# Attention, layer norm and a routed expert layer on one core: the four picked rows of a token summed as two halves inside the expert loop

## The chip, the cores and the metric

One core of a Trainium2 chip runs the whole program as one launch. The metric is the device time of an execution in microseconds (us). Between two versions, about 2% is what a measurement of this kernel can tell from no change.

## What is computed

4,096 tokens of width 256 go through one layer of attention with a residual and a layer norm, and then through a routed expert layer with a shared expert, a residual and a second layer norm. The reference, cut to the part that the change is about:

```python
topk_idx, topk_w = _route(tokens, router_weight, router_bias)    # 4 of 32 experts for each token
gate_vals = silu(einsum('th,eih->tei', tokens, gate_w))
up_vals = einsum('th,eih->tei', tokens, up_w)
expert_out = einsum('tei,ehi->teh', gate_vals * up_vals, down_w)
sel = take_along_axis(expert_out, topk_idx[:, :, None], axis=1)
mixed = (sel * topk_w[:, :, None]).sum(1)                        # the sum over a token's 4 picks
x = layernorm(x + mixed + shared)
```

## The kernel before

**Stages.** Attention, routing and the shared expert run over 8 chunks of 512 tokens, in an order written out by hand. Each token's row is scattered four times into a DRAM tensor `xs` (`expert_rows`), sorted by expert. Then comes the expert loop, and after it a closing stage that adds what is left of the picked rows, takes the moments and writes the output.

**The expert loop.** A tile is 128 rows of one expert. Two tiles are a pair, four are a group (`quad` in the code), which is thus two pairs, `par` 0 and `par` 1; below, a pair is also called half a group. There are 34 groups here. Buffers of a pair are double, chosen by `par`. For pair n the engines do this, each in its own program order:

- SP (`load_rows`, line 506) loads the two tiles of a pair into `xt[par]`, 132 KB each. It waits until pair n-2 has been transposed (`cX_ps`) and until DVE has copied that pair's ids and weights (`cmeta`).
- PE (`pairs`) transposes pair n+1 (line 1355), runs the 16 gate and up matmuls of pair n (line 996) and the down matmuls of pair n-1 (line 996).
- ACT (`pairs`) copies ids and weights (`keep_meta`, line 930), copies the transposed rows of pair n+1 (line 912), takes the silu of pair n (line 938) and scales the result of pair n-1 into `y_sb` (`copy_y`, line 921). `copy_y` waits until the scatter that last read this buffer, that of pair n-3, has landed (`y_scattered`).
- DVE (`pairs`) copies the ids and weights of pair n+1 (`copy_meta`, line 1825), multiplies silu by up (`hT`, line 1851), makes the ids of pair n-1 (`label_rows`, line 1842, which waits for the same scatter), then looks up the experts of pair n+2 in registers (`find_weights`, lines 295 and 1829) and copies their weights into `ws` (`copy_weights`, line 1834).
- POOL (`scatter_y`, line 608) scatters the two result tiles to the DRAM tensor `z` (`pick_rows`), four rows for each token.

**Early sums.** In the last 17 groups the loop also sums picked rows of the first 16 token tiles (of 32), one tile in each group: their results are known to be complete by then. `quads_with_ends` calls `load_early` on ACT behind each half of the groups from the 17th from the end to the second from the end; in half 0 it issues one DMA of 512 KB (line 951), 128 rows of 4 KB (four picks of 256 floats), into `early_z`, which lies over `wsgu_sb`. On DVE the function `beside` is called in `pairs` between `label_rows` and `find_weights`. `sum_halves(tile)` in half 1 of the same group waits for the load and adds 512 columns to 512 columns (line 1867). `sum_row(tile)` in half 0 of the next group adds 256 to 256 (line 1872), waits for that, and adds the result to the residual row in `sx` (line 1875). After the load of a tile the buffer is free once line 1867 has run (`e_free`), half a group before the next load.

The closing stage on DVE begins when all 16 tiles are summed (`e_sum`), and the picked rows of the other 16 tiles are loaded by SP after the loop (`load_picks`, line 525).

Of the kernel before, what the change touches and what calls it, by code (L numbers as in the profile page):

```python
# [9 lines left out]
ALU = mybir.AluOpType  # L10
# [3 lines left out]
P = 128  # L14
NTOK, DM = 4096, 256
# [5 lines left out]
TOPK, NGROUP = 4, 4  # L21
# [5 lines left out]
CT = 512  # L27
# [8 lines left out]
FIRST_TILES = FIRST_CHUNKS * TPC  # L36
# [34 lines left out]
SUM_LAG = 3  # L71
SUM_GROUPS = FIRST_TILES
# [12 lines left out]
def build(nc, xT, x, wqkv, wfc, wr, rbias, wsgu, wsd, wgu, wd, out):  # L85
# [7 lines left out]
    with ExitStack() as ctx:  # L93
# [6 lines left out]
        def sem(name):  # L100
            return ctx.enter_context(nc.semaphore(name))
# [140 lines left out]
        hT = [over(prod, 8 * DM + 4 * ROW + (4 + 2 * i) * P, 2 * P) for i in range(2)]  # L242
        ws = [over(prod, 8 * DM + 4 * ROW + 8 * P + i * 2 * KC * 2 * EI, 2, KC * 2 * EI) for i in range(2)]

        early_z = wsgu_sb.rearrange("p k c -> p (k c)")
        early_sum = wqkv_sb.rearrange("p k c -> p (k c)")[:, 2 * CT:2 * CT + 2 * DM]
        zt = {g: over(wgu_sb, (g - 5) * TPC * TOPK * DM, TPC * TOPK, DM).rearrange("p (t k) c -> p t k c", k=TOPK)
              for g in range(FIRST_CHUNKS + 1, CH)}
        zt[FIRST_CHUNKS] = over(stage.rearrange("p t k r -> p (t k r)"), 0, TPC * TOPK, DM)\
# [11 lines left out]
        b tabT tab_ready  # L261
        xt0 xt1 cX_ps cX_copied cmeta kept ws_ready ids_ready cgu_ps cth_ready ch_ready cy_ps cy_copied
        yscat0 yscat1
        e_free e_z e_half e_sum
        d_a d_ps dst_ready dmv_ready dveps_ready dstd_ready drstd_ready dnm_ready o2_ready stored""".split()
        S = {name: sem(name) for name in SEMS}
        xT_loaded = [S["xT_loaded0"], S["xT_loaded1"]]
# [1 line left out]
        scattered = [S[f"scat{i}"] for i in range(TPC)]  # L269
        xt_loaded = [S["xt0"], S["xt1"]]  # L270
        y_scattered = [S["yscat0"], S["yscat1"]]
        z_loaded = {g: [sem(f"z_loaded{g}_{t}") for t in range(TPC)] for g in range(FIRST_CHUNKS, CH)}

        NSMALL = 5 * 16
# [361 lines left out]
        def _(act):  # L636
# [305 lines left out]
                    first = isinstance(n, int) and n < 3  # L942
                    copy_y(n - 1, 1 - par, None if first else (quad * 32 if par else quad * 32 - 32))

            def load_early(quad, tile, par):
                if par:
                    return
                act.wait_ge(S["e_free"], tile + 1)
                for i in range(2):
                    act.wait_ge(y_scattered[i], quad * 32 - 32 * SUM_LAG)  # L950
                act.dma_start(early_z[:, :], z.rearrange("(n k) c -> n (k c)", k=TOPK)[bass.ds(tile * P, P), :])\
                    .then_inc(S["e_z"], 16)

            copy_xT(0, 0)
            quads_with_ends(act, quads, pairs, load_early)
# [466 lines left out]
        def _(dve):  # L1422
# [421 lines left out]
            def pairs(quad, par, has_prev, has_next, more=True, beside=None):  # L1844
                n = quad * 2 + par
                if has_next:
                    copy_meta(n + 1, 1 - par, quad + par)
                dve.wait_ge(S["cth_ready"], n + 1)
                if not (isinstance(n, int) and n < 2):
                    dve.wait_ge(S["cy_ps"], n - 1)  # L1850
                dve.tensor_tensor(hT[par][:, :], cth[par][:, :], banks[par][:, 2 * P:4 * P], ALU.mult)\  # L1851
                    .then_inc(S["ch_ready"], 1)
                if has_prev:
                    first = isinstance(n, int) and n < 3
                    label_rows(n - 1, 1 - par, None if first else (quad * 32 if par else quad * 32 - 32))
                if beside:
                    beside()
                if more:
                    found = find_weights(quad + 1, 2 * par)
                    dve.wait_ge(S["cgu_ps"], n + 1)  # L1860
                    copy_weights(par, found)

            def sum_halves(tile):
                dve.wait_ge(S["e_z"], tile * 16 + 16)
                if not isinstance(tile, int):
                    dve.wait_ge(S["e_sum"], tile)
                dve.tensor_tensor(early_sum[:, :], early_z[:, 0:2 * DM], early_z[:, 2 * DM:], ALU.add)\
                    .then_inc(S["e_free"], 1)

            def sum_row(tile):  # L1870
                dve.wait_ge(S["e_free"], tile + 2)
                dve.tensor_tensor(early_sum[:, 0:DM], early_sum[:, 0:DM], early_sum[:, DM:], ALU.add)\
                    .then_inc(S["e_half"], 1)
                dve.wait_ge(S["e_half"], tile + 1)
                dve.tensor_tensor(sx[:, bass.ds(tile * DM, DM)], sx[:, bass.ds(tile * DM, DM)], early_sum[:, 0:DM],
                                  ALU.add).then_inc(S["e_sum"], 1)

            dve.memset(slot_first[:, :], 0.0).then_inc(S["e_free"], 1)
            copy_meta(0, 0, 0)
            dve.wait_ge(S["big_w"], 16 * NBIG)  # L1880
            copy_weights(0, find_weights(0, 0))
            copy_weights(1, find_weights(0, 2))
            pairs(0, 0, False, True)
            pairs(0, 1, True, True)
            with dve.Fori(1, quads - SUM_START) as quad:
                pairs(quad, 0, True, True)
                pairs(quad, 1, True, True)
            first = dve.snap(dve.to_reg(quads - SUM_START))
            pairs(first, 0, True, True)
            pairs(first, 1, True, True, beside=lambda: sum_halves(0))  # L1890
            with dve.Fori(1, SUM_GROUPS) as tile:
                quad = dve.snap(dve.to_reg(quads - SUM_START + tile))
                pairs(quad, 0, True, True, beside=lambda: sum_row(tile - 1))
                pairs(quad, 1, True, True, beside=lambda: sum_halves(tile))
            pairs(quads - 1, 0, True, True, False, lambda: sum_row(SUM_GROUPS - 1))
            pairs(quads - 1, 1, True, False, False)
            label_rows(quads * 2 - 1, 1, None, True)


# [27 lines left out]
                dve.tensor_scalar(dveps[g][:, first:last], dmv[g][:, first:last, 1], EPS, None, ALU.add)\  # L1927
                    .then_inc(S["dveps_ready"], 1)

            dve.wait_ge(S["e_sum"], FIRST_TILES)  # L1930
            moments(0, 0, TPC)
            moments(1, 0, TPC)
            add_picks(4, range(TPC))
# [74 lines left out]
```

## Time and profile before

| | us |
|---|---|
| median of 3 runs | 597.07 |
| the runs | 588.22, 597.07, 598.96 |
| profiled execution, its own time | 589.56 |
| its span, first to last instruction | 587.8 |
| PE busy (matmuls) | 540.7 (92%) |
| DVE busy | 343.5 (58%) |
| ACT busy | 301.2 (51%) |
| POOL busy | 281.3 (48%) |

The profiled execution lies near the fastest of the three runs. Differences inside it are read against its own span; only at the end is the change carried over to the median. Busy shares are means over stages with different limits, so what matters below is read inside the expert loop, from about 316 us to about 547 us of the span. In a timeline row the first two numbers are the start and the duration in us; `x16` counts instructions merged into one row, and the bracket at its end gives how long the engine was idle before it and what ended that.

### The profile page before, as it was taken

To read this page: it belongs to the slowest core of one execution; us is meant where nothing else is said; L and a number is where in the kernel's file an instruction comes from. 1 tells how busy PE (TensorE), PEld (TensorE's weight loads), DVE (VectorE), ACT (ScalarE), POOL (GpSimd) and SP (SyncE) were. 2 spreads that over 40 slices of the span, in tenths; PEclk is the share of its full clock that TensorE was granted. 3 is DMA by queue.
4 is the path that set the end of the run, shared out by engine and by line. 5 is a ranking of instruction groups with operands and counts; after the bars stand their busy time and mean duration, and the time that the engine had idled before them with its cause. 6 is when DMAs were issued, how large, how long until landed. Compare 5 with 4: busy or idle time off the path is not lost.

```text
span 587.8 us, 16300 instructions
## 1 busy us (share of the span) xinstructions
PE 540.7 (92%) x4820; PEld 418.7 (71%) x4821; DVE 343.5 (58%) x1167; ACT 301.2 (51%) x641; POOL 281.3 (48%) x293
## 2 busy tenths in 40 slices
PE   5989999999999999999888999999988888888894
PEld 2445668677666766775437999999977777778783
DVE  2032647697985987678834444444455555555865
ACT  1324462766747665343214666666555555545454
POOL 5000000564677766667741666666655555555400
PEclk9989999999999999999988999999999999989999
DMA  7999987897799799799523454555666666667498
GB/s 258 248 220 229 249 237 192 246 282 223 245 259 288 243 311 398 272 383 344 183 92 91 136 159 160 163 168 179 200 209 213 212 203 213 209 201 254 162 383 293
DMA packets 125821, 135.35 MB, mean 230 GB/s; under 512 B 76872, under 2 KB 107087, under 8 KB 125136
## 3 DMA queue, kind: packets, MB, share of 16 engines
q1 hardware_dynamic: 105984, 87.53, 50.8%
q0 software_dynamic: 12672, 34.10, 15.3%
q10 hardware_dynamic: 7120, 13.13, 7.2%
q8 instruction: 27, 0.44, 0.3%
q14 instruction: 18, 0.15, 0.1%
HBM read 74.79 MB, written 60.96 MB: 231 GB/s over the span
## 4 chain that ended last, share of the span: by engine, by line
PE 56%; DMA 21%; issue 6%; DVE 4%; SPq 4%; POOL 3%; ACT 3%; DVEq 1%; ACTq 1%; POOLq 0%
PE bank L996 51%; DMA prod<-expert_rows 4%; DMA o_slots<-wgu_sb 4%; DMA pick_rows<-prod,ids 4%; PE bank L1355 4%; DMA wd_sb<-o_slots 3%; DMA wgu_sb<-pick_rows 3%; DMA wsgu_sb<-pick_rows 2%; POOL expert_rows L574 1%; ACT sx L965 1%; SPq L364 1%; SPq L355 1%; POOL pick_rows L608 1%; SPq L525 1%; PE bank L1044 1%
## 5 line engine op out<-in xcount | busy, mean ns | idle before, releaser
L608 POOL DMA_INDIRECT pick_rows<-prod,ids x134 | 133.6, 997 | 114.5 <-ACT prod L921 68.8
L574 POOL DMA_INDIRECT expert_rows<-stage,pos x128 | 128.6, 1004 | 57.3 <-issue 35.0
L996 PE MATMUL bank<-prod 128*128 128x128 f32 x1088 | 135.2, 278 | 1.0 <-DVE prod L1834 1.0
L996 PEld LDWEIGHTS bank<-prod 128*128 128x128 f32 x1088 | 128.9, 194 | 1.6 <-ACT prod L912 1.2
L996 PE MATMUL bank<-wd_sb,wqkv_sb 128*128 128x512 f32 x192 | 92.1, 616 | 7.0 <-DMA wqkv_sb<-in_wqkv 6.2
L1834 DVE COPY prod<-wgu_sb 128x512 f32 x136 | 52.8, 430 | 62.2 <-issue 42.0
L921 ACT ACTIVATE prod<-bank,kept 128x256 f32<-128x256 f32 x136 | 57.0, 470 | 50.0 <-PE bank L996 27.2
L996 PE MATMUL bank<-wd_sb,prod 128*128 x272 | 70.9, 384 | 1.3 <-DVE prod L1851 1.3
L996 PEld LDWEIGHTS bank<-wgu_sb 128*32 128x32 f32 x2048 | 58.7, 136 | 17.5 <-issue 14.2
L996 PE MATMUL bank<-wgu_sb 128*32 128x64 f32 x2048 | 65.8, 296 | 2.9 <-DMA wgu_sb<-k_slots 2.9
L996 PEld LDWEIGHTS bank<-wd_sb,wqkv_sb 128*128 128x128 f32 x192 | 35.3, 196 | 42.5 <-issue 36.4
L1355 PE MATMUL bank<-ident,prod 128*128 128x128 f32 x272 | 42.1, 278 | 19.1 <-DMA prod<-expert_rows 17.0
L567 POOL TENSOR_TENSOR rstdt<-vepst,neg_half 128x4 f32<-128x4 f32 x8 | 9.0, 1129 | 99.7 <-DVE vepst L1456 99.7
L1355 PEld LDWEIGHTS bank<-ident,prod 128*128 128x128 f32 x272 | 33.0, 143 | 31.6 <-issue 22.2
L1851 DVE TENSOR_TENSOR prod<-prod,bank 128x256 f32<-128x256 f32 x68 | 28.5, 419 | 42.0 <-ACT prod L938 41.8
L996 PEld LDWEIGHTS bank<-wd_sb,prod 128*128 128x128 f32 x272 | 47.0, 193 | 5.4 <-issue 1.7
L996 PE MATMUL bank<-prod,wsgu_sb 128*128 128x512 f32 x96 | 45.2, 618 | 3.4 <-DVE hsT L1523 3.4
L938 ACT ACTIVATE prod<-bank 128x256 f32<-128x256 f32 x68 | 26.0, 383 | 42.5 <-PE bank L996 41.9
L912 ACT ACTIVATE prod<-bank 128x512 f32<-128x512 f32 x68 | 40.6, 597 | 3.5 <-PE bank L1355 2.9
L1474 DVE TENSOR_REDUCE smax<-bank 128x32 f32<-128x512 f32 x16 | 10.9, 681 | 48.0 <-PE bank L996 48.0
L653 ACT ACTIVATE stage<-sx 128x1024 f32<-128x1024 f32 x32 | 34.1, 1065 | 9.3 <-DMA expert_rows<-stage,pos 6.7
L996 PEld LDWEIGHTS bank<-prod,wsgu_sb 128*128 128x128 f32 x96 | 18.2, 197 | 24.8 <-issue 19.6
(168 smaller groups left out, 699.2 us busy)
## 6 DMA issues: line engine op xcount, KB each, us to landing
prod<-expert_rows SPq DMA_DIRECT2D x136, 132.0 KB
wsgu_sb<-pick_rows ACTq DMA_DIRECT2D x16, 512.0 KB
wgu_sb<-pick_rows SPq DMA_DIRECT2D x12, 512.0 KB, 11.0
wgu_sb<-in_wgu SPq DMA_DIRECT2D x2, 2560.0 KB, 13.0
expert_rows<-pad_rows SPq DMA_DIRECT2D x4, 1056.0 KB, 19.4
wd_sb<-in_xT SPq DMA_DIRECT2D x8, 512.0 KB, 4.8
q_slots<-wd_sb SPq DMA_DIRECT2D x16, 256.0 KB, 4.2
k_slots<-wd_sb SPq DMA_DIRECT2D x16, 256.0 KB
```

The source lines that it names most:

```text
L567: pool.tensor_tensor(rstdt[:, :], vepst[:, :], neg_half[:, :], ALU.pow).then_inc(S["rstd_ready"], 1)
L574: pool.indirect_dma_start(xs, bass.IndirectOffsetOnAxis(ap=pos[e % 2][:, i, k:k + 1], axis=0), stage[:, i, k, :], None, bounds_check=XROWS ...
L608: pool.indirect_dma_start(z, bass.IndirectOffsetOnAxis(ap=index[:, j:j + 1], axis=0), rows[:, j, :], None, bounds_check=TOPK * NTOK - 1, o ...
L653: act.activation(stage[:, i, :, 0:DM], x1_of(e)[:, i, :].unsqueeze(1).broadcast_to([P, TOPK, DM]), ACT.Copy)
L912: act.activation(xtT[par][:, :], banks[2][:, :], ACT.Copy).then_inc(S["cX_copied"], 1)
L921: last = act.activation(to[:, j, :], banks[6 + par][:, j * DM:(j + 1) * DM], ACT.Copy, scale=kept[par][:, j, 1:2])
L938: act.activation(cth[par][:, :], banks[par][:, 0:2 * P], ACT.Silu)\
L996: return pe.matmul(dst, lhsT, rhs, start=(k == 0), stop=(k == n - 1))
L1355: last = pe.transpose(banks[2][:, c:c + P], xt[par][:, j, k * P:(k + 1) * P], ident[:, :])
L1474: dve.tensor_reduce(smax[:, hf, :], score_view(hf), AX, ALU.max).then_inc(S["smax"], 1)
L1834: last = dve.tensor_copy(ws[par][:, j, :], wgu_sb[:, bass.ds(found[j], KC * 2 * EI)])
L1851: dve.tensor_tensor(hT[par][:, :], cth[par][:, :], banks[par][:, 2 * P:4 * P], ALU.mult)\
```

## The change

`early_z` becomes two buffers of 512 columns, each for two of the four picks of a row. `load_early` now issues a DMA in both halves of a group, 256 KB each (128 rows of 2 KB). `sum_halves` and `sum_row` are replaced by `sum_half`, called in both halves: it waits for its load, adds 256 columns to 256, waits for that, and adds the result to the row in `sx`. The sums of a tile now stand in the group behind the one in which its loads are issued, each in the same half as its load was, so a load is waited for one whole group later. The load of tile t waits until `sum_half` of tile t-1 has read the buffer, which happens in the same half group. Columns added and bytes loaded are the same in all. On DVE the group that stood by itself (`first`) is gone and the last half of the last group now has a sum.

```diff
-        early_z = wsgu_sb.rearrange("p k c -> p (k c)")
-        early_sum = wqkv_sb.rearrange("p k c -> p (k c)")[:, 2 * CT:2 * CT + 2 * DM]
+        early_z = [over(wsgu_sb.rearrange("p k c -> p (k c)"), h * 2 * DM, 2, DM) for h in range(2)]
+        early_sum = wqkv_sb.rearrange("p k c -> p (k c)")[:, 2 * CT:2 * CT + DM]
...
-            def load_early(quad, tile, par):
-                if par:
-                    return
-                act.wait_ge(S["e_free"], tile + 1)
-                for i in range(2):
-                    act.wait_ge(y_scattered[i], quad * 32 - 32 * SUM_LAG)
-                act.dma_start(early_z[:, :], z.rearrange("(n k) c -> n (k c)", k=TOPK)[bass.ds(tile * P, P), :])\
-                    .then_inc(S["e_z"], 16)
+            def load_early(quad, tile, half):
+                act.wait_ge(S["e_half"], tile * 2 + half)
+                if half == 0:
+                    for i in range(2):
+                        act.wait_ge(y_scattered[i], quad * 32 - 32 * SUM_LAG)
+                act.dma_start(early_z[half][:, :, 0:DM],
+                              z.rearrange("(n k) c -> n k c", k=TOPK)[bass.ds(tile * P, P),
+                                                                      2 * half:2 * half + 2, :])\
+                    .then_inc(early_landed[half], 16)
...
-            def sum_halves(tile):
-                dve.wait_ge(S["e_z"], tile * 16 + 16)
-                if not isinstance(tile, int):
-                    dve.wait_ge(S["e_sum"], tile)
-                dve.tensor_tensor(early_sum[:, :], early_z[:, 0:2 * DM], early_z[:, 2 * DM:], ALU.add)\
-                    .then_inc(S["e_free"], 1)
-
-            def sum_row(tile):
-                dve.wait_ge(S["e_free"], tile + 2)
-                dve.tensor_tensor(early_sum[:, 0:DM], early_sum[:, 0:DM], early_sum[:, DM:], ALU.add)\
+            def sum_half(tile, half):
+                dve.wait_ge(early_landed[half], tile * 16 + 16)
+                dve.wait_ge(S["e_sum"], tile * 2 + half)
+                dve.tensor_tensor(early_sum[:, :], early_z[half][:, 0, 0:DM], early_z[half][:, 1, 0:DM], ALU.add)\
                     .then_inc(S["e_half"], 1)
-                dve.wait_ge(S["e_half"], tile + 1)
-                dve.tensor_tensor(sx[:, bass.ds(tile * DM, DM)], sx[:, bass.ds(tile * DM, DM)], early_sum[:, 0:DM],
+                dve.wait_ge(S["e_half"], tile * 2 + half + 2)
+                dve.tensor_tensor(sx[:, bass.ds(tile * DM, DM)], sx[:, bass.ds(tile * DM, DM)], early_sum[:, :],
                                   ALU.add).then_inc(S["e_sum"], 1)
...
-            with dve.Fori(1, quads - SUM_START) as quad:
+            with dve.Fori(1, quads - SUM_GROUPS) as quad:
                 pairs(quad, 0, True, True)
                 pairs(quad, 1, True, True)
-            first = dve.snap(dve.to_reg(quads - SUM_START))
-            pairs(first, 0, True, True)
-            pairs(first, 1, True, True, beside=lambda: sum_halves(0))
-            with dve.Fori(1, SUM_GROUPS) as tile:
-                quad = dve.snap(dve.to_reg(quads - SUM_START + tile))
-                pairs(quad, 0, True, True, beside=lambda: sum_row(tile - 1))
-                pairs(quad, 1, True, True, beside=lambda: sum_halves(tile))
-            pairs(quads - 1, 0, True, True, False, lambda: sum_row(SUM_GROUPS - 1))
-            pairs(quads - 1, 1, True, False, False)
+            with dve.Fori(0, SUM_GROUPS - 1) as tile:
+                quad = dve.snap(dve.to_reg(quads - SUM_GROUPS + tile))
+                pairs(quad, 0, True, True, beside=lambda: sum_half(tile, 0))
+                pairs(quad, 1, True, True, beside=lambda: sum_half(tile, 1))
+            pairs(quads - 1, 0, True, True, False, lambda: sum_half(SUM_GROUPS - 1, 0))
+            pairs(quads - 1, 1, True, False, False, lambda: sum_half(SUM_GROUPS - 1, 1))
             label_rows(quads * 2 - 1, 1, None, True)
```

## Rows read from the trace of the kernel before

**Rows 1.** The page: the span.
```profile
span 587.8 us, 16300 instructions
```

**Rows 2.** Windows: us, busy us of PE, PEld, DVE, ACT, POOL (instructions), clock, DMA share, GB/s.
```profile
330.00:348.50 18.50, 18.50 (x146) 17.59 (x145) 8.03 (x31) 11.77 (x31) 11.67 (x12) 1.00 0.47 148
...
488.00:503.00 15.00, 12.81 (x96) 11.61 (x96) 8.08 (x26) 8.06 (x21) 8.29 (x9) 1.00 0.68 214
```

**Rows 3.** The tile `wsgu_sb` (`early_z`): shortest, median, longest ns, first and last start in us.
```profile
L951 ACTq DMA_DIRECT2D wsgu_sb<-pick_rows x16: 344/344/372, 421.8 to 535.1; - x16
```

**Rows 4.** Timeline of PE without early loads: transposes of two pairs.
```profile
384.08 0.60 PE L1355 MATMUL bank<-ident,prod 128*128 128x128 f32 x4
...
387.17 0.60 PE L1355 MATMUL bank<-ident,prod 128*128 128x128 f32 x4
```

**Rows 5.** Timeline of DVE without early loads.
```profile
383.92 0.42 DVE L1851 TENSOR_TENSOR prod<-prod,bank 128x256 f32<-128x256 f32 x1 [0.99 <-ACT prod L938]
...
386.01 0.16 DVE L1825 COPY meta<-prod 128x4 f32<-128x4 f32 x1
386.92 0.42 DVE L1851 TENSOR_TENSOR prod<-prod,bank 128x256 f32<-128x256 f32 x1 [0.74 <-ACT prod L938]
```

**Rows 6.** Timeline of DVE with early loads: a group, and one later row.
```profile
481.26 0.42 DVE L1851 TENSOR_TENSOR prod<-prod,bank 128x256 f32<-128x256 f32 x1 [0.94 <-ACT prod L938]
...
482.25 0.43 DVE L1875 TENSOR_TENSOR sx<-sx,wqkv_sb 128x256 f32 x1 [0.17 <-DVE wqkv_sb L1872]
483.85 0.78 DVE L1834 COPY prod<-wgu_sb 128x512 f32 x2 [1.17 <-PE bank L996]
484.55 0.15 DVE L1825 COPY meta<-prod 128x4 f32<-128x4 f32 x1
484.61 0.41 DVE L1851 TENSOR_TENSOR prod<-prod,bank 128x256 f32<-128x256 f32 x1
...
486.07 0.69 DVE L1867 TENSOR_TENSOR wqkv_sb<-wsgu_sb 128x512 f32<-128x512 f32 x1 [0.97 <-DMA wsgu_sb<-pick_rows]
...
488.29 0.16 DVE L1825 COPY meta<-prod 128x4 f32<-128x4 f32 x1
...
537.34 0.83 DVE L1834 COPY prod<-wgu_sb 128x512 f32 x2 [1.48 <-issue]
```

**Rows 7.** Waits from 421 to 548 us: us in total, times, longest us.
```profile
ACT prod L921 <- DMA pick_rows<-prod,ids: 22.5, 16, 2.8
...
PE bank L1355 <- DMA prod<-expert_rows: 16.7, 13, 2.2
...
DVE wqkv_sb L1867 <- DMA wsgu_sb<-pick_rows: 6.0, 7, 1.3
```

**Rows 8.** Timeline of PE with early loads: transposes.
```profile
481.42 0.60 PE L1355 MATMUL bank<-ident,prod 128*128 128x128 f32 x4
...
493.30 0.65 PE L1355 MATMUL bank<-ident,prod 128*128 128x128 f32 x4 [1.74 <-DMA prod<-expert_rows]
```

**Rows 9.** The chain that ended last, with early loads: start us, us from issue to landing.
```profile
472.62 5.22 DMA pick_rows<-prod,ids
...
489.31 3.86 DMA prod<-expert_rows
...
515.38 2.26 DMA prod<-expert_rows
```

**Rows 10.** DMA from 421 to 536 us: a queue's share of 16 engines' time; issues.
```profile
q1 hardware_dynamic: 8674, 8.15, 24.8%
q10 hardware_dynamic: 2160, 7.87, 23.7%
...
prod<-expert_rows SPq DMA_DIRECT2D x61, 132.0 KB
```

**Rows 11.** The page, costliest groups: busy us, mean ns of one | idle us before, releaser.
```profile
L608 POOL DMA_INDIRECT pick_rows<-prod,ids x134 | 133.6, 997 | 114.5 <-ACT prod L921 68.8
...
L921 ACT ACTIVATE prod<-bank,kept 128x256 f32<-128x256 f32 x136 | 57.0, 470 | 50.0 <-PE bank L996 27.2
```

More of the change, by code:

```diff
@@ L263, in build @@
         yscat0 yscat1
-        e_free e_z e_half e_sum
+        e_z0 e_z1 e_half e_sum
         d_a d_ps dst_ready dmv_ready dveps_ready dstd_ready drstd_ready dnm_ready o2_ready stored""".split()
@@ L271, in build @@
         y_scattered = [S["yscat0"], S["yscat1"]]
+        early_landed = [S["e_z0"], S["e_z1"]]
         z_loaded = {g: [sem(f"z_loaded{g}_{t}") for t in range(TPC)] for g in range(FIRST_CHUNKS, CH)}
@@ L1861, in pairs @@
                     copy_weights(par, found)
-            def sum_halves(tile):
-                dve.wait_ge(S["e_z"], tile * 16 + 16)
-                if not isinstance(tile, int):
-                    dve.wait_ge(S["e_sum"], tile)
-                dve.tensor_tensor(early_sum[:, :], early_z[:, 0:2 * DM], early_z[:, 2 * DM:], ALU.add)\
-                    .then_inc(S["e_free"], 1)
-            def sum_row(tile):
-                dve.wait_ge(S["e_free"], tile + 2)
-                dve.tensor_tensor(early_sum[:, 0:DM], early_sum[:, 0:DM], early_sum[:, DM:], ALU.add)\
+            def sum_half(tile, half):
+                dve.wait_ge(early_landed[half], tile * 16 + 16)
+                dve.wait_ge(S["e_sum"], tile * 2 + half)
+                dve.tensor_tensor(early_sum[:, :], early_z[half][:, 0, 0:DM], early_z[half][:, 1, 0:DM], ALU.add)\
                     .then_inc(S["e_half"], 1)
-                dve.wait_ge(S["e_half"], tile + 1)
-                dve.tensor_tensor(sx[:, bass.ds(tile * DM, DM)], sx[:, bass.ds(tile * DM, DM)], early_sum[:, 0:DM],
+                dve.wait_ge(S["e_half"], tile * 2 + half + 2)
+                dve.tensor_tensor(sx[:, bass.ds(tile * DM, DM)], sx[:, bass.ds(tile * DM, DM)], early_sum[:, :],
                                   ALU.add).then_inc(S["e_sum"], 1)
-            dve.memset(slot_first[:, :], 0.0).then_inc(S["e_free"], 1)
+            dve.memset(slot_first[:, :], 0.0).then_inc(S["e_half"], 1)
             copy_meta(0, 0, 0)
@@ L1928, in moments @@
                     .then_inc(S["dveps_ready"], 1)
-            dve.wait_ge(S["e_sum"], FIRST_TILES)
+            dve.wait_ge(S["e_sum"], 2 * FIRST_TILES)
             moments(0, 0, TPC)
```

## Prediction

> **What bounds the kernel now.** I read the page first: PE is busy 92% of a span of 587.8 us [rows 1], so the question is where in the expert loop it is not. The windows answer that [rows 2]. Without early loads PE is busy for all of 18.50 us at a DMA share of 0.47; with them it is busy 12.81 of 15.00 us at 0.68. The timeline gives the pace of the undisturbed stretch: transposes of successive pairs start 387.17 - 384.08 = 3.09 us apart [rows 4], so a group takes 6.18 us and PE sets it. With early loads the 16 DMAs run from 421.8 to 535.1 us [rows 3], 113.3 us for 15 groups or 7.55 us each. A group with an early load therefore costs 1.37 us more than one without, 15 x 1.37 = 20.6 us in all. That is everything the change can win back in these groups.
>
> The waits tell who stands still in that stretch [rows 7]: `copy_y` on ACT for a scatter (22.5 us in 16 waits), PE's transposes for expert rows (16.7 us in 13), and DVE's line 1867 for the early load itself (6.0 us in 7). The totals overlap in time and may not be added. The timelines show how they hang together. DVE waits 0.97 us for the early load at 486.07 and so copies ids and weights (`copy_meta`) only at 488.29 [rows 6]. SP may load into that buffer only after this copy, and its second DMA is out at 489.31; it takes 3.86 us [rows 9], beside an early load, and PE stands 1.74 us before it transposes at 493.30 [rows 8]. The reader is to see that DVE is off PE's path only while `copy_meta` comes early enough.
>
> **The loop that sets the pace.** From a pair's transposes to those three pairs later, with the rows of before: transposes to `hT` 484.61 - 481.42 = 3.19; `hT` to `copy_meta` 488.29 - 484.61 = 3.68; `copy_meta` to the last issue 489.31 - 488.29 = 1.02; landing 3.86; then 0.13 to 493.30. The sum is 11.88 us, as measured [rows 6, 8, 9], instead of 3 x 3.09 = 9.27. Undisturbed it is 386.92 - 384.08 = 2.84, 386.01 - 383.92 = 2.09, 1.02, 2.26 for a landing that met little traffic [rows 9] and 0.13: 8.34 us, a slack of 0.93 us [rows 4, 5].
>
> **The change, part by part.**
>
> *The wait for the load goes.* The early load is waited for a group later. The longest idle time seen for it is 1.3 us [rows 7], so 6 to 7 us more notice covers it, and the 256 KB loads are no longer than the 512 KB ones. Removed: up to 6.0 us of DVE idle time; what of this reaches PE is in the loop sum below, not on top of it.
>
> *DVE's work.* Before, one half of a group has one add of 512 columns (0.69 us), the other two adds of 256 (0.42 and 0.43) with a wait of 0.17 between [rows 6]. After, both halves have the latter. The first form cost little when its data were there. The second is heavy: with `sum_row`, `hT` to `copy_meta` takes 484.55 - 481.26 = 3.29 us, against 2.09 without [rows 5, 6], as the register work for the next weights is not hidden behind the adds (1.17 us idle before line 1834). `hT` to the next `hT` is 484.61 - 481.26 = 3.35 us, which is more than PE's 3.09. So DVE alone holds each of these halves at 3.35 us or more, a group at 6.70. That is the lower bound. The upper one is a longer register stretch: 1.48 us instead of 1.17 at 537.34 [rows 6] makes 3.66. One more wait against a register in each half lies between these.
>
> *The loads.* Early loads take 23.7% of 115 us x 16 engines, 27.3 us for 15 of them: 1.8 us of all engines each. The expert rows take 24.8%, 28.5 us for 61 DMAs of 132 KB, 0.47 us each, and so 0.91 us per 256 KB in packets of 1 KB [rows 10]. Two halves with packets of 2 KB then cost the engines the same 1.8 us as one whole; no bytes are saved. What changes is the burst. A load of expert rows issued beside a whole one takes 3.86 us instead of 2.26, +1.6; beside a half I take half of that, 3.06 us, for every pair now instead of mostly every second. The bounds are 2.26 (it slips past) and 3.86 (no relief).
>
> *The pace after.* The loop is 2.84 + 3.29 + 1.02 + 3.06 + 0.13 = 10.34 us for three pairs, 3.45 us a pair. With a landing of 2.26 it is 3.18, so DVE's 3.35 holds; with 3.86 it is 3.71. As DVE's floor and this loop lie 0.1 us apart and each has scatter, I take 3.50: a group of 7.00 us, 0.55 less than now.
>
> *The scatters.* `copy_y` and `label_rows` wait for scatters that take up to 5.22 us beside a whole load [rows 9]. Beside a half one, the same +0.9 of engine time instead of +1.8 brings them down to about 4.3. Ahead of the landing stand two copies of 0.47 us and two issues of 1.0 us [rows 11], an estimated 2.9 us, so the slowest would need 7.2 us of a two-pair time of 7.0, the others less. I count nothing for it beyond the 3.50.
>
> *What ACT waits for.* Each early load now waits for the first add on DVE in the same half. That ends at 482.25 - 0.17 = 482.08, 0.82 us behind the start of `hT` [rows 6], while ACT has its two copies of 0.47 us to do [rows 11]. Behind it on ACT are `keep_meta`, the copy of the transposed rows and the next silu; POOL and PE wait for those. ACT's 8.06 us busy of 15.00 [rows 2] is the cover; without it the price is what DVE is late, some 0.1 to 0.3 us a half. The additional 16 issues (0.34 us each [rows 3]) run while ACT's datapath copies: nothing.
>
> *Ends.* The first group with loads now has no sums; it had about 6.2 us already: nothing. The last group gets sums in both halves, but its last `label_rows` needs only be ready when the down matmuls and `copy_y` are: nothing, or the two adds and their wait, 1.0 us, if that cover is gone. One group less written out on DVE: nothing.
>
> **Sum.** 15 x (7.55 - 7.00) = 8.3 us less: span 579.5, own time 589.56 - 8.3 = 581.3, that is -1.4%. The profiled execution was 7.5 us faster than the median of the runs, 597.07. Carried over, 597.07 - 8.3 = 588.8; I say 589.
>
> The Trainium skill, page "DMA: Bandwidth & Descriptors", section "Bandwidth", speaks against this change: batch DMAs to 1 MiB or more, since a DMA costs about 2.0 us plus its bytes at 436 GB/s. By that, 512 KB in one takes an estimated 3.2 us and in two 5.2, and if the fixed part held the engines the change would cost 2.0 us a group. The trace doesn't bear that out: DMAs of 132 KB hold the engines for 0.47 us each, so the fixed part must be latency, which is hidden here.
>
> **Rivals.**
>
> 1. *Almost the whole loss goes.* Half bursts fall below the slack of 0.93 us and DVE's register work hides behind its waits; a group takes 6.2 to 6.5 us. For it: half of +1.6 is 0.8, below 0.93. Against it: `copy_meta` itself comes 1.2 us later in each half, and 3.35 us is a plain row. Saves 15 x 1.2 = 18: 579 on the median.
> 2. *Nothing changes.* The bytes are the same and the DMA share of 0.68 is what sets the pace; `copy_y` waits move to other places. For it: 22.5 us of waits for scatters, no part of DVE. A group stays at 7.4 to 7.6: 595 to 598.
> 3. *Slower: DVE becomes the bound.* The place is the stretch between `label_rows` and `copy_meta`, in each half; it decides from 7.55 / 2 = 3.78 us per half. The rows give 3.35 to 3.66; a scatter waited for in `label_rows` in front of it adds directly, as there is no light half left in which DVE catches up. At 3.95 us a group takes 7.90: +5 us, 602.
> 4. *Small DMAs hold the engines* (the engines busy 2.0 us more a group than the 1.8 above): with a DMA share of 0.68 + 2.0 / 7.55 = 0.94 nothing would be left for scatter, and a group would take at least 1 to 2 us more: 612 to 627. Only engine times of 0.47 us for 132 KB stand against it, and they do so plainly.
>
> **Chances.** Forecast (4 to 12 us less) 0.54, rival 1 0.12, rival 2 0.20, rival 3 0.12, rival 4 0.02. About 2%, 12 us, is what a measurement of this kernel can tell from no change. Faster by more than that takes rival 1 and DVE's floor of 3.35 (15 x 0.85 = 12.8 us): 0.12 + 0.13 = 0.25. Slower by over 2% is rival 4 and the tail of rival 3, with the runs of before 11 us apart: 0.08. The rest, 0.67, lies within. The range: below, rival 1 all but its end, 577; above, rival 3, 602. Forecast's own: 585 to 593.
>
> **What would show it.** Right: no row of DVE waiting for the early load; issues of early loads 3.5 us apart; `hT` to `hT` of 3.35 us or more with hardly any idle time for silu; PE's waits for expert rows many and short (0.3 to 0.4 us) instead of 13 long ones; expert rows landing in about 3.1 us. Wrong: landings near 3.9 us, waits of `copy_y` for scatters still at 22 us, or `hT` to `hT` above 3.78 us. The same DMA share with two queues' times unchanged would confirm the cost of the loads; a share above 0.8 would refute it.

## The result

| | before | changed |
|---|---|---|
| median of 20 runs, us | 596.84 | 584.82 |
| lowest to highest, us | 588.22 to 601.75 | 582.45 to 590.98 |
| ratio of the runs | | 0.9886, 95% interval 0.9846 to 0.9925 |
| profiled execution's span, us | 587.8 | 584.4 |

The changed kernel is about 1.1% faster, clear of chance and inside the 2% that stood for "no change". In a second comparison the ratio was 0.9866 (0.9817 to 0.9915). The two medians lie 2.0% apart, more than the ratio says: the ratio compares the means of the fast runs alone, those within 1.5% of their kernel's fastest, which leaves out 9 of the 20 runs of before and none of the changed kernel. The two first traces lie only 3.4 us (0.6%) apart. Part of the kernel before's spread is what its stalls do to TensorE's clock, which comes below; its first trace had little of that.

**The profile after.** First the early loads (tile `wsgu_sb`: count, shortest, median and longest ns, first and last start in us) and the first add that reads them:

```profile
L951 ACTq DMA_DIRECT2D wsgu_sb<-pick_rows x32: 339/344/363, 423.1 to 535.4; - x32
L1868 DVE TENSOR_TENSOR wqkv_sb<-wsgu_sb x32: 411/419/426, 429.4 to 543.6; 128x256 f32<-128x256 f32 x32
```

From the first to the last of 32 loads there are 15.5 groups: (535.4 - 423.1) / 15.5 = 7.24 us a group, instead of 7.55 [rows 3]. The forecast was 7.00. From here on the pace of a group is worked out like this for every kernel with early loads.

These means hide how unlike the groups of the kernel before are. Here are its issues of early loads, one for each group, and below them those of half 0 in the changed kernel (timelines of ACT):

```profile
421.82 0.36 ACTq L951 DMA_DIRECT2D wsgu_sb<-pick_rows  x1
428.00 0.35 ACTq L951 DMA_DIRECT2D wsgu_sb<-pick_rows  x1
436.79 0.34 ACTq L951 DMA_DIRECT2D wsgu_sb<-pick_rows  x1
442.99 0.37 ACTq L951 DMA_DIRECT2D wsgu_sb<-pick_rows  x1
451.69 0.34 ACTq L951 DMA_DIRECT2D wsgu_sb<-pick_rows  x1
```

```profile
439.18 0.34 ACTq L951 DMA_DIRECT2D wsgu_sb<-pick_rows  x1
...
446.21 0.34 ACTq L951 DMA_DIRECT2D wsgu_sb<-pick_rows  x1
...
453.56 0.34 ACTq L951 DMA_DIRECT2D wsgu_sb<-pick_rows  x1
```

In the kernel before, short and long groups take turns: 6.18, 8.79, 6.20, 8.70 us, and so on to the end. The short ones run at the pace without early loads (6.18); the loss of 1.37 us a group is one of about 2.6 us in every second group. The changed kernel has nearly even groups: of the 15 from one issue in half 0 to the next, the median is 7.03 us and the longest 9.01. This was not in the forecast, which took 7.55 us as the time of each group.

The waits from 421 to 548 us (total us, times, longest us), which answer to [rows 7]:

```profile
PE bank L1357 <- DMA prod<-expert_rows: 10.3, 15, 1.7
ACT prod L922 <- DMA pick_rows<-prod,ids: 8.8, 7, 3.3
DVE ids L1844 <- DMA pick_rows<-prod,ids: 6.2, 4, 2.6
```

No row is left in which DVE waits for an early load; it was 6.0 us. PE's waits for expert rows fell from 16.7 to 10.3 us, `copy_y`'s for scatters from 22.5 to 8.8. New are waits of ACT ahead of `keep_meta`, two rows of which are these:

```profile
ACT kept L931 <- issue: 8.5, 6, 1.8
ACT kept L931 <- DMA pick_rows<-prod,ids: 7.3, 11, 1.2
```

With the two other rows of that line they come to 25.2 us in 31 waits, against 1.7 us in 5 before. An ACT that is late by itself also has less to wait for in `copy_y`.

The timeline of DVE, two halves of a group, answers to [rows 6]:

```profile
438.05 0.42 DVE L1853 TENSOR_TENSOR prod<-prod,bank 128x256 f32<-128x256 f32 x1
...
439.02 0.43 DVE L1871 TENSOR_TENSOR sx<-sx,wqkv_sb 128x256 f32 x1
440.89 0.76 DVE L1836 COPY prod<-wgu_sb 128x512 f32 x2 [1.44 <-PE bank L998]
441.57 0.22 DVE L1827 COPY meta<-prod 128x4 f32<-128x4 f32 x1
441.64 0.41 DVE L1853 TENSOR_TENSOR prod<-prod,bank 128x256 f32<-128x256 f32 x1
...
444.01 0.76 DVE L1836 COPY prod<-wgu_sb 128x512 f32 x2 [1.10 <-PE bank L998]
444.88 0.17 DVE L1827 COPY meta<-prod 128x4 f32<-128x4 f32 x1
```

`hT` to `copy_meta` takes 441.57 - 438.05 = 3.52 us in one half and 444.88 - 441.64 = 3.24 in the other, where the forecast had 3.29 for both. The idle time in front of line 1836, in which DVE looks up the experts in registers, is longer in half 0 (1.44 us, against 1.10). The row names PE, but the matmuls that this line waits for are those that `hT` needed already.

The DMA queues from 421 to 536 us answer to [rows 10], and the chain (start us, us) to [rows 9]:

```profile
q1 hardware_dynamic: 9092, 8.89, 29.5%
q10 hardware_dynamic: 4453, 8.11, 23.4%
```

```profile
477.55 3.60 DMA prod<-expert_rows
...
491.92 2.54 DMA prod<-expert_rows
```

Queue q10 took 23.4% of the engines' time for 8.11 MB; before it was 23.7% for 7.87 MB. So two DMAs of 256 KB in packets of 2 KB cost the engines what one of 512 KB did, as forecast, and small transfers do not hold them. The queue of the expert rows, q1, did not stay the same. From 428 to 528 us, where it carries nothing else, it took 28.2% of the engines' time for 7.30 MB, against 24.7% for 7.18 MB in the kernel before: 14% more time for 2% more bytes.

### The profile page after: what moved, and what is told of

It reads as the page before. It is cut to its first block, busy times and chain, and to the rows that moved or that the text cites. A ratio compares the mean times of both kernels' runs of the same rounds, so it can differ in the third digit from the quotient of the medians.

```text
span 584.4 us, 16411 instructions
## 1 busy us (share of the span) xinstructions
PE 542.0 (93%) x4820; PEld 419.2 (72%) x4821; DVE 346.0 (59%) x1183; ACT 299.5 (51%) x641; POOL 281.2 (48%) x293
## 4 chain that ended last, share of the span: by engine, by line
PE 59%; DMA 17%; issue 7%; SPq 4%; POOL 4%; DVE 3%; ACT 2%; DVEq 2%; POOLq 0%; ACTq 0%
PE bank L998 54%; DMA prod<-expert_rows 5%; PE bank L1357 4%; POOL expert_rows L575 4%; DMA o_slots<-wgu_sb 3%; DMA wd_sb<-o_slots 2%; DMA wgu_sb<-pick_rows 2%; DMA pick_rows<-prod,ids 1%; ACT sx L967 1%; SPq L514 1%; SPq L356 1%; DMA expert_rows<-stage,pos 1%; DVEq L296 1%; DMA wqkv_sb<-in_wqkv 1%; PE bank L1046 1%
## 5 line engine op out<-in xcount | busy, mean ns | idle before, releaser
L1836 DVE COPY prod<-wgu_sb 128x512 f32 x136 | 54.1, 440 | 67.9 <-issue 52.0
```

Of the source, the lines that this page charges most:

```text
L1836: last = dve.tensor_copy(ws[par][:, j, :], wgu_sb[:, bass.ds(found[j], KC * 2 * EI)])
```

## The experiments

Ratios are against the kernel before on the same chip, with 95% intervals. PE's busy time is that of the 100 us from 428 to 528 us of each trace; matmuls at a low clock count in full. "Single groups" are the shortest, the median and the longest of the 15 between issues of early loads (of half 0, where there are two). The kernel with sums only has no such issues: its groups are counted from add to add, which takes in the last group, 8.88 us. Counted so, the changed kernel is at (543.6 - 429.4) / 15.5 = 7.37 us.

| kernel | ratio (95%) | median us | us per group | single groups | PE busy |
|---|---|---|---|---|---|
| before, first trace | | 596.84 | 7.55 | 6.18, 6.40, 10.42 | 85.1 |
| before again | 1.0031 (0.9991 to 1.007) | 598.36 | 7.83 | 6.18, 6.86, 10.73 | 85.9 |
| changed, first trace | 0.9886 (0.9846 to 0.9925) | 584.82 | 7.24 | 6.66, 7.03, 9.01 | 89.1 |
| changed again | 0.9866 (0.9817 to 0.9915) | 585.65 | 7.21 | 6.64, 7.05, 8.56 | 89.7 |
| halves, old notice | 0.9899 (0.9851 to 0.9947) | 588.90 | 7.37 | 6.18, 7.44, 8.26 | 87.1 |
| whole, a group's notice | 0.989 (0.9845 to 0.9934) | 587.25 | 7.35 | 6.66, 7.13, 9.42 | 87.8 |
| halved loads, no sums | 0.9885 (0.9812 to 0.9959) | 587.99 | 7.34 | 6.61, 7.17, 8.31 | 88.2 |
| whole loads, no sums | 1.0013 (0.9969 to 1.0057) | 596.67 | 7.81 | 6.18, 7.76, 9.99 | 83.5 |
| sums, no loads | 0.9782 (0.972 to 0.9844) | 579.73 | 6.99 | 6.66, 6.94, 8.88 | 95.2 |
| adds apart | 0.9917 (0.9884 to 0.995) | 588.88 | 7.33 | 6.45, 7.36, 8.17 | 86.5 |
| changed + tile scatters | 0.98 (0.9742 to 0.9858) | 582.25 | 7.10 | 6.68, 7.03, 7.51 | 90.6 |
| adds apart + tile scatters | 0.9818 (0.9766 to 0.987) | 583.68 | 6.90 | 6.21, 6.81, 7.98 | 92.5 |
| before + tile scatters | 0.9925 (0.9885 to 0.9965) | 589.69 | 7.66 | 6.22, 6.44, 10.78 | 85.3 |

### The two kernels again

No edit: the kernel before and the changed one beside it.

> The kernel before once more, beside itself: what difference two equal kernels show here, and a second trace of it. Ratio 1.00, within 1% either way; its runs lie between 588 and 602 us. In its trace the groups with an early load take 7.4 to 7.8 us each (7.55 in the first trace); if they take over 7.8 us, the first trace was one of the quick executions and the change is worth more than its two traces show.

> The changed kernel once more, on the same chip as the three others. Theory (the wait for the early load is gone and the bursts are halved): ratio 0.98 to 0.99, groups of 7.0 to 7.3 us in its trace. Rival (nothing but chance of one execution): ratio 0.995 or more.

Two equal kernels differed by 0.3%. The second trace of before has a span of 598.2 us against 587.8 of the first and 7.83 us a group; the changed kernel's second trace has 583.3 us and 7.21. The change is thus worth 0.3 to 0.6 us a group by the traces, depending on which execution of before is taken.

Part of what makes before vary shows in its windows (length, busy us of PE, PEld, DVE, ACT, POOL, granted clock, DMA share, GB/s), here of its second trace:

```profile
498.00:501.50 3.50, 1.06 (x8) 0.66 (x8) 2.03 (x6) 0.97 (x3) 0.98 (x1) 1.00 0.96 334
501.50:505.00 3.50, 3.50 (x19) 3.43 (x18) 0.88 (x3) 0.82 (x3) 2.05 (x2) 0.51 0.39 113
...
515.00:518.60 3.60, 1.38 (x11) 0.98 (x11) 2.02 (x6) 1.31 (x4) 0.98 (x1) 1.00 0.92 329
518.60:522.00 3.40, 3.40 (x17) 3.22 (x16) 1.05 (x4) 0.70 (x2) 1.07 (x1) 0.50 0.43 129
```

and in the timeline of PE of the same trace:

```profile
500.86 0.65 PE L1355 MATMUL bank<-ident,prod 128*128 128x128 f32 x4 [2.44 <-DMA prod<-expert_rows]
501.35 3.44 PE L996 MATMUL bank<-prod 128*128 128x128 f32 x16
...
505.63 0.60 PE L1355 MATMUL bank<-ident,prod 128*128 128x128 f32 x4
506.07 1.95 PE L996 MATMUL bank<-prod 128*128 128x128 f32 x16
```

PE stands 2.44 us for expert rows, while the DMA share is 0.96, and in the stretch behind that the granted clock is 0.51: the lower of its two levels, 1.2 instead of 2.4 GHz. Sixteen matmuls take 3.44 us instead of 1.95. The same happens at 518.6 and at 535.7 us in this trace, and once in the first trace of before, at 524.6 us (0.51, after an idle time of 2.09 us). Each costs about 1.7 us on top of the stall: 2.80 + 1.88 us of matmuls instead of 1.95 + 1.03 in the first trace. The groups show the same price: with a drop they take 10.42 to 10.73 us, without one the long ones take 8.44 to 8.98. In neither trace of the changed kernel does the clock drop between 421 and 540 us; PE's longest idle time there is 1.69 us. Outside this stretch it does: near 312 to 317 us in both traces, as in the first trace of before, and at 542 us in the second. The runs bear out that the clock is part of before's spread: of the 57 runs of before that the ratios below rest on, the lowest third (592.4 us on the mean) had a mean granted clock of 0.984, the highest (597.8 us) one of 0.979. This was not in the forecast.

### Notice without halves, halves without notice

```diff
 # halves, old notice: the changed kernel, half 0 added in half 1 of the same group, half 1 in half 0 of the next
-                pairs(quad, 0, True, True, beside=lambda: sum_half(tile, 0))
-                pairs(quad, 1, True, True, beside=lambda: sum_half(tile, 1))
+                pairs(quad, 0, True, True, beside=lambda: sum_half(tile - 1, 1))
+                pairs(quad, 1, True, True, beside=lambda: sum_half(tile, 0))
```

> The changed kernel with only the point of adding moved back: two loads of 256 KB as after the change, each added half a group later as before (half 0 in half 1 of the same group, half 1 in half 0 of the next). The number of adds on DVE is that of the change. If the halved bursts bring the gain: ratio 0.985 to 0.99, like the changed kernel, since a load of 256 KB lands in 2.5 to 3.9 us and half a group is 3.5 us, so DVE waits little. If the longer notice brings it: DVE waits 0.3 us or more in most halves, and the ratio is 0.995 to 1.01.

```diff
 # whole, a group's notice: the kernel before, both sums in the group behind the load
-                pairs(quad, 0, True, True, beside=lambda: sum_row(tile - 1))
-                pairs(quad, 1, True, True, beside=lambda: sum_halves(tile))
+                pairs(quad, 0, True, True, beside=lambda: sum_halves(tile))
+                pairs(quad, 1, True, True, beside=lambda: sum_row(tile))
```

> The kernel before with only the point of adding moved: one load of 512 KB a group as before, its first add (512 columns) in half 0 of the next group and the other two in half 1, so that the load has a whole group. DVE's work is that of the kernel before. If the longer notice brings the gain: ratio 0.985 to 0.99 or better, since DVE has one light half. If the halved bursts bring it: ratio 0.995 to 1.005, expert rows still landing in 3.9 us beside each load, and only the 6.0 us of DVE's waits for the early load gone from the waits.

Each part alone brings most of the gain, 1.0% and 1.1%, and both together 1.1 to 1.3%; the intervals of all overlap. In both kernels the ratio is the one expected if the part tested brings the gain, so neither is the only cause, and the parts are not additive. That both relieve the same loop, once by making DVE punctual, once by making the traffic smoother, is a reading that no run separates. The single groups add something to it: with whole loads and a group's notice short and long groups no longer take turns (6.66 to 7.33 us for 11 of 15), with halves and the old notice they still do for the most part (6.2 to 7.4 and 7.6 to 8.3). With halves and the old notice DVE also still waits for its loads:

```profile
DVE wqkv_sb L1868 <- DMA wsgu_sb<-pick_rows: 6.3, 9, 3.8
```

### Loads alone, sums alone

```diff
 # halved loads, no sums (whole loads: the same edit in the kernel "whole, a group's notice")
-                dve.tensor_tensor(early_sum[:, :], early_z[half][:, 0, 0:DM], early_z[half][:, 1, 0:DM], ALU.add)\
-                    .then_inc(S["e_half"], 1)
-                dve.wait_ge(S["e_half"], tile * 2 + half + 2)
-                dve.tensor_tensor(sx[:, bass.ds(tile * DM, DM)], sx[:, bass.ds(tile * DM, DM)], early_sum[:, :],
-                                  ALU.add).then_inc(S["e_sum"], 1)
+                dve.memset(slot_first[:, 0:1], 0.0).then_inc(S["e_half"], 1)
+                dve.memset(slot_first[:, 1:2], 0.0).then_inc(S["e_sum"], 1)
 # sums, no loads
-                act.dma_start(early_z[half][:, :, 0:DM], ...)
-                dve.wait_ge(early_landed[half], tile * 16 + 16)
```

> The changed kernel with the sums left out: the 32 loads of 256 KB stay, the two adds of each half are replaced by two writes of one column, so the early token tiles lack their picked rows. It shows what the halved loads cost without DVE's work. If the loads (not DVE) hold the loop: groups stay at 6.9 to 7.3 us, ratio 0.985. If DVE's stretch from hT to copy_meta holds it (theory: 1.2 us later against a slack of 0.93): hT to copy_meta falls to about 2.3 us and groups to 6.2 to 6.4 us, ratio about 0.97.

> The same without the sums, but with the 16 loads of 512 KB, waited for a group later: the early token tiles lack their picked rows. Beside the halved loads it shows the burst alone. If a whole burst is worth a stall of its own: groups 0.3 us or more longer than with halves, expert rows beside it landing in 3.9 us against 3.1. If the slack of 0.93 us covers both, no difference between the two, both near 6.2 to 6.4 us.

> The changed kernel with its early loads left out: DVE adds what lies in the buffer, so the early token tiles get wrong picked rows. It shows DVE's work without the traffic. Theory (DVE's floor): groups of 6.7 to 6.8 us, hT to hT 3.35 us, PE with idle time of some 0.3 us a half; ratio 0.98. Rival (only the traffic costs): groups 6.2 us, ratio 0.965 to 0.97.

These three take the loss apart. The sums without traffic need 6.99 us a group ((537.0 - 428.7) / 15.5 from line 1863, the first add), with a median of 6.94, near the forecast floor of 6.70; the timeline of DVE shows where the rest is:

```profile
483.66 0.42 DVE L1849 TENSOR_TENSOR prod<-prod,bank 128x256 f32<-128x256 f32 x1
...
487.05 0.42 DVE L1849 TENSOR_TENSOR prod<-prod,bank 128x256 f32<-128x256 f32 x1
...
490.56 0.42 DVE L1849 TENSOR_TENSOR prod<-prod,bank 128x256 f32<-128x256 f32 x1
```

`hT` to `hT` is 3.39 and 3.51 us: 3.35 and a little more. That the rest is one more wait against a register and lookups that vary is likely, but not shown.

The halved loads without any sums need 7.34 us, hardly less or more than the whole change. Taking most of 1 us of DVE's work out of each half gained nothing: of the two expectations that came true in which the loads hold the loop, not the 6.2 to 6.4 us of the other. The waits of that kernel point to what held it:

```profile
ACT prod L922 <- DMA pick_rows<-prod,ids: 31.1, 20, 2.9
DVE ids L1844 <- DMA pick_rows<-prod,ids: 18.9, 17, 2.3
```

`copy_y` and `label_rows` wait for scatters. DVE's waits only moved from its own work to the landings. The whole loads without sums are at 7.81 us and at the time of the kernel before (ratio 1.0013), and the granted clock drops in that trace too (0.96 on the mean of 428 to 528 us, with 1.00 for the halves), three times, after PE had stood 2.94, 2.69 and 2.48 us:

```profile
428.00:528.00 100.00, 83.48 (x602) 75.64 (x601) 38.46 (x152) 49.97 (x127) 51.08 (x52) 0.96 0.67 207
```

Between whole and halved bursts, with no sums in either, lie 0.47 us a group and 1.3% by the ratios (medians 587.99 and 596.67 us, intervals that do not touch: 0.9812 to 0.9959 and 0.9969 to 1.0057). The burst is a cause of its own. At about 1.7 us each, the three clock drops are an estimated 0.3 of the 0.47 us: most of what the whole burst costs here goes through the clock.

### The adds taken apart

```diff
 # adds apart: first add ahead of hT, second behind label_rows
                 if has_next:
                     copy_meta(n + 1, 1 - par, quad + par)
+                if beside:
+                    add_half(*beside)
                 dve.wait_ge(S["cth_ready"], n + 1)
...
                 if beside:
-                    beside()
+                    add_sum(*beside)
```

> The changed kernel with the two adds of a half taken apart: the first stands ahead of the hT multiply, where DVE waits for silu anyway, the second behind label_rows, so that no completion is waited for between them and the register work runs while the second add does. Same adds, same loads. Theory: hT to copy_meta falls from 3.3 to about 2.5 us and groups from 7.1 to about 6.5 us; 15 x 0.6 = 9 us, ratio 0.97 against before. Rival (the traffic holds the loop, not DVE): groups stay at 7 us or more, ratio 0.985.

The rival won. `hT` to `copy_meta` did fall (a half at 485.64 to 487.95, 2.31 us), but the group stayed at 7.33 us. The trace of this kernel shows the loop that holds it without DVE's work in the way (timelines of POOL and ACT):

```profile
484.10 0.97 POOL L609 DMA_INDIRECT pick_rows<-prod,ids  x1 [1.80 <-ACT prod L922]
485.37 1.20 POOL L609 DMA_INDIRECT pick_rows<-prod,ids  x1 [0.30 <-issue]
```

```profile
482.41 0.47 ACT L922 ACTIVATE prod<-bank,kept 128x256 f32<-128x256 f32 x1 [1.70 <-DMA pick_rows<-prod,ids]
...
482.78 0.47 ACT L922 ACTIVATE prod<-bank,kept 128x256 f32<-128x256 f32 x1
...
489.57 0.47 ACT L922 ACTIVATE prod<-bank,kept 128x256 f32<-128x256 f32 x1 [1.50 <-DMA pick_rows<-prod,ids]
```

```profile
485.37 4.17 DMA pick_rows<-prod,ids
```

ACT begins `copy_y` at 482.41, is done at 483.25, POOL issues the first scatter at 484.10 and the second at 485.37, that one lands 4.17 us later (the chain's row), and ACT begins the next copy into the same buffer at 489.57. Those are 7.16 us for two pairs, which is a group: 2.96 up to the last issue, 4.17 for the landing and 0.03 until the next copy.

### A semaphore for each tile's scatter

```diff
 # tile scatters: copy_y waits, and POOL issues, for each of the two tiles by itself
-                if old is not None:
-                    act.wait_ge(y_scattered[par], old)
                 for j in range(2):
-                    last = act.activation(to[:, j, :], banks[6 + par][:, j * DM:(j + 1) * DM], ACT.Copy,
-                                          scale=kept[par][:, j, 1:2])
-                last.then_inc(S["cy_copied"], 1)
+                    if old is not None:
+                        act.wait_ge(y_scattered[par][j], old)
+                    act.activation(to[:, j, :], banks[6 + par][:, j * DM:(j + 1) * DM], ACT.Copy,
+                                   scale=kept[par][:, j, 1:2]).then_inc(S["cy_copied"], 1)
...
-                wait_apart(pool, S["cy_copied"], pair * 2 + par + 1)
                 for j in range(2):
+                    wait_apart(pool, S["cy_copied"], pair * 4 + par * 2 + j + 1)
```

> The changed kernel with the scatter of each result tile on a semaphore of its own: copy_y waits for the scatter of the tile that it overwrites only, and POOL issues a tile's scatter when that tile is copied, not when both are. This shortens the loop copy, issue, landing, copy by one copy (0.84 - 0.2 us) without touching DVE or the early loads. Theory A (the scatters' loop of 7.2 us for two pairs holds the changed kernel, DVE's 6.9 stands right behind it): groups fall from 7.2 to 6.9 or 7.0 us, ratio about 0.98 against before. Theory B (only DVE's stretch holds it): no difference to the changed kernel, 0.987. Theory C (POOL's added waits make its issues later): ratio 0.99 or more.

> The same with the adds taken apart as in adds_apart, so that both loops are shorter: scatters' 6.4 to 6.5 us for two pairs, DVE's about 5.5 to 6.2 us a group. Theory A: groups of 6.5 to 6.8 us, 15 x 0.5 = 7 us below the changed kernel, ratio 0.975 against before. If neither loop is what holds it but the traffic itself: groups stay at 7.1 to 7.4 us, ratio 0.99 as adds_apart.

> The kernel before with the scatters on a semaphore for each tile, and nothing else. If the scatters' loop was already what one half of the loss in the kernel before came from (copy_y waited 22.5 us for scatters there, landings of 5.2 us beside a whole load make a loop of 8.2 us): groups fall from 7.55 by some 0.3 us, ratio 0.985 to 0.99. If the expert rows, held back by DVE, set the pace alone: ratio 0.995 to 1.005.

With the adds apart the shorter scatter loop takes a group from 7.33 to 6.90 us and the ratio from 0.9917 to 0.9818; the intervals (0.9884 to 0.995, 0.9766 to 0.987) do not touch. `copy_y`'s waits for scatters go from 32.0 us to nearly nothing:

```profile
ACT prod L924 <- DMA pick_rows<-prod,ids: 1.9, 5, 0.6
```

So the scatters' loop held that kernel, in every group: the median falls from 7.36 to 6.81 us. The 6.5 to 6.8 us a group and the ratio of 0.975 that were expected were not quite reached.

On the changed kernel the same edit takes a group from 7.2 to 7.10 us and gives 582.25 us, ratio 0.98 (0.9742 to 0.9858): the fastest kernel here that computes the whole result, though its interval overlaps that of the changed kernel. The median of its groups, 7.03 us, is that of the changed kernel; what is gone is the long group near the start. On the kernel before it gives 0.9925, below 1 by its interval, although the pace in its one trace (7.66 us, two clock drops in it) is not below the 7.55 and 7.83 of the two traces of before. `copy_y`'s waits for scatters fall there from 22.5 to 6.6 us, but short and long groups still take turns. That scatters cost the kernel before something is thus supported by the time and not by the pace of the trace.

## Why the prediction was right, and where it was off

- **What could be won, 1.37 us a group.** Right as a mean; it is 2.6 us in every second group of the kernel before and nothing in the others. No kernel went below a mean of 6.90 us a group.
- **The wait for the load goes.** Right: no such wait is left. The longer notice taken alone (whole, a group's notice) is worth most of the gain, which fits a loss that runs through a late `copy_meta`.
- **DVE's floor of 3.35 us a half.** Nearly right: 3.39 to 3.51 in the kernel without loads, a median of 6.94 us a group instead of 6.70. The term is mis-sized by 0.1 us a half; the extra wait that had been named and not counted may be the reason.
- **The loads cost the engines the same.** Right: 23.4% for 8.11 MB against 23.7% for 7.87 MB, though the expert rows' queue took more time for each byte than before. The "Bandwidth" section of the Trainium skill's page "DMA: Bandwidth & Descriptors", on batching to 1 MiB, was weighed and set aside, and the runs bear that out: the halved bursts beat the whole ones by 1.3% with no sums beside them. The cost of about 2.0 us plus the bytes that the prediction names with it stands in another section of that page, "Anatomy of one DMA — SWDGE (gpsimd) path", for DMAs issued from GpSimd; the early loads are issued from ACT. The section "Queues, rings and completion order" of the same page says that an engine takes turns between queues by the packet, a packet there being some 9 to 17 descriptors. Whether the packets of 2 KB and 4 KB that the profile counts are of that kind is shown by no run here, so that rule stays unproven as the reason.
- **Expert rows landing in 3.06 us.** Not borne out where it can be seen: the eight landings of expert rows in the chain from 421 to 540 us take 2.30 to 3.93 us, 3.33 on the mean, and the seven of the kernel before 2.26 to 4.01, 3.43 on the mean. These are only those that something waited for. PE's waits did not become many and short as forecast either: 15 of 0.7 us on the mean, the longest 1.7.
- **The pace, 3.50 us a pair.** Right for the typical group: the median is 7.03 and 7.05 us in the two traces, 3.52 a pair. The means, 7.24 and 7.21, lie above it through single long groups, 9.01 and 8.56 us near the start and some of 7.5 to 7.9. The term that was too small is the one on the scatters, "I count nothing for it", and with it the landing of "about 4.3". In the long group of the first trace a scatter landed in 5.19 us and `label_rows` stood for it (the chain, then the timeline of DVE):

```profile
429.74 5.19 DMA pick_rows<-prod,ids
```

```profile
435.01 0.17 DVE L1844 CAST ids<-kept 128x2 uint32<-128x2 f32 x1 [1.85 <-DMA pick_rows<-prod,ids]
```

- **The scatters' loop.** The forecast's own sum, 2.9 + 4.3 = 7.2 us for the slowest, was measured as 7.16, but in the kernel with the adds apart, where this loop holds every group. In the changed kernel nine of 15 groups are shorter than that, so there it can hold some and not the typical one; DVE's 6.94 us comes nearest to the 7.03.
- **ACT's wait on the first add.** It does occur: ACT stands 25.2 us ahead of `keep_meta`, which follows `load_early` in its program, instead of 1.7. How much of it is the first add is unclear. The profile's view of line 1868 puts 8.1 us in 6 waits down to it, its rows of line 931 only 1.8 in 2. The 7.3 us put down to scatters need not be that either, as `load_early` asks only for scatters of three groups earlier. The kernel with sums only has 17.0 us of this idle time and is the fastest of all; the one with the adds apart has 7.6, gained nothing by it, and waits 32.0 us for scatters in `copy_y` instead. The wait was not taken away by itself, so its cost stays open, and so does that of the 16 more issues, which the forecast put at nothing.
- **The sum.** 8.3 us less were forecast. The ratio, 0.9886, is 6.8 us of 592.7, the mean of before that it rests on; the medians differ by 12.0 us. For the profiled execution 581.3 us was forecast and 586.14 measured, 3.4 less instead of 8.3. The traces' pace gives 15 x (7.55 - 7.24) = 4.7 us from the first two traces and 15 x (7.83 - 7.21) = 9.3 from the second two. In these stand one and three clock drops of before, an estimated 1.7 and 5.1 us; without them the change saves 3.0 and 4.2 us. So the loops that the forecast reasons about gave a third to a half of what it promised, and the clock, of which it says nothing, gave 1.7 to 5.1 us on top. That the total came out near 8.3 us is in part luck, and the step that the median moves by what the quick execution moves did not hold.
- **Rivals.** "Almost the whole loss goes" fell on DVE's floor; "nothing changes" was half right in its mechanism (the scatters) and wrong in its result; "DVE becomes the bound" was right about the place and wrong about the result: DVE's typical 6.94 us lies just below the 7.03 measured; "small DMAs hold the engines" did not occur.

**What stays open.** In both traces of the changed kernel and in that with whole loads and a group's notice, one group near the start of the sums takes 8.6 to 9.4 us. In the changed kernel's first trace it goes with the scatter that lands in 5.19 us; why that one lands so late is not known. Why short and long groups take turns in the kernel before is not shown either. And why the halved loads without sums are no faster in ratio than the full change (0.9885 and 0.9886), although they lack DVE's work, is explained by the scatters' loop only as far as one trace shows. Group times, waits and clock drops of the experiments come from one trace each.

## What to carry to other kernels

When one engine is made punctual and one transfer smooth, work out every loop through a double buffer, and not only the one that holds now: copy, issue, landing and copy again is a loop of its own, and its landing time must be taken beside the traffic, not alone. With several loops close together, taking work off one of them can gain nothing, as the adds taken apart showed. A background load was better here in two bursts than in one, with other transfers waited for, although DMA time and bytes stayed the same. And list the single groups before working from their mean: here a mean of 7.55 us stood for 6.2 and 8.8 in turn.

## What the runs showed of the hardware

TensorE's granted clock fell to 1.2 GHz inside the loop after stalls of 2.09, 2.22, 2.44 and 2.45 us in the traces of before, 2.48 to 2.94 us in the one with whole loads and no sums, and 1.98 and 2.01 us in the one of before with tile scatters. PE was busy throughout the stretch at the lower clock, which so cost about 1.7 us more: a stall of 2.09 us in the first trace of before came to some 3.8. The clock did not fall after each such stall. In the first trace of before PE stood 2.19 us before 478.28, and in the second 2.21 us before 485.62, and both times it ran on at full clock:

```profile
485.62 0.65 PE L1355 MATMUL bank<-ident,prod 128*128 128x128 f32 x4 [2.21 <-DMA prod<-expert_rows]
486.11 1.95 PE L996 MATMUL bank<-prod 128*128 128x128 f32 x16
```

A change that only evens out short stalls can thus win more than the stalls' own time.
